# Cross network on one Trainium2 core: one layer-one chunk in two passes, bank 2 added whole, the sum over d in fp32r

## The reference

```python
x0 = xk = e                                    # (1024, 39, 16)
for W in (f0, f1, f2):
    z = einsum('bfd,bgd->bfgd', x0, xk)         # all pairs of x0 and xk
    xk = einsum('bpd,pm->bmd', z.reshape(b, f * g, d), W)
    outs.append(xk)
z = sum(concatenate(outs, axis=1), axis=-1)     # sum over d: (1024, 384)
h = concatenate([z, dense_ctx], axis=1)
h = maximum(h @ W_top1 + b_top1, 0)
h = maximum(h @ W_top2 + b_top2, 0)
y = h @ W_top3
```

## Time and profile before

| | |
|---|---|
| median of 3 runs | 1281.71 us (1281.46 to 1281.8) |
| the profiled execution's own time | 1282.15 us |
| its span | 1280.3 us |
| PE busy | 1247.0 us, 97% |
| DVE busy | 1038.5 us, 81% |
| POOL busy | 951.5 us, 74% |
| ACT busy | 751.1 us, 59% |

### The profile page before, as it was taken

How to read it: one execution, slowest core, us unless ns; L and a number is a source line. 1 busy time by engine, 2 the same in 40 slices (tenths; PEclk the granted TensorE clock), 3 DMA queues, 4 the chain that set the end, 5 groups by cost and what they waited for, 6 DMA issues and landing times.

```text
span 1280.3 us, 19891 instructions
## 1 busy us (share of the span) xinstructions
PE 1247.0 (97%) x5493; PEld 963.6 (75%) x5493; DVE 1038.5 (81%) x3346; ACT 751.1 (59%) x2422; POOL 951.5 (74%) x844
## 2 busy tenths in 40 slices
PE   1999999999999999999999999999999999999999
PEld 0677778777787778777787777877787777877765
DVE  4789896898868996889969888699978898788830
ACT  4456664666646665666646666466656666466641
POOL 6578886788868886788868888588867888675640
PEclk9999999999999999999999999999999999999999
DMA  7632222122212221122221222222221222111000
GB/s 174 180 102 61 66 69 61 45 54 68 62 57 69 68 60 40 50 61 68 69 54 38 68 61 66 61 68 61 53 48 51 66 69 68 47 44 50 1 1 1
DMA packets 121764, 78.69 MB, mean 61 GB/s; under 512 B 77436, under 2 KB 89826, under 8 KB 121652
## 3 DMA queue, kind: packets, MB, share of 16 engines
q1 hardware_dynamic: 107418, 73.69, 20.4%
q0 software_dynamic: 10240, 2.64, 2.4%
q10 hardware_dynamic: 3994, 1.09, 0.4%
HBM read 18.50 MB, written 2.63 MB: 16 GB/s over the span
## 4 chain that ended last, share of the span: by engine, by line
PE 97%; DMA 1%; POOL 1%; issue 0%; ACTq 0%; ACT 0%; DVE 0%; SPq 0%
PE ps L499 23%; PE ps L503 22%; PE ps L500 22%; PE ps L479 14%; PE ps L526 6%; PE ps L515 5%; PE ps L582 2%; PE ps L592 1%; PE ps L462 1%; POOL x_in L393 1%; DMA x_in<-in_tables,row_at 0%; PE ps L599 0%; ACTq L272 0%; DMA x_rows<-x_in 0%; DMA ids_now<-in_ids 0%
## 5 line engine op out<-in xcount | busy, mean ns | idle before, releaser
L823 DVE SCALAR_TENSOR_TENSOR terms<-ps,x_scal,terms 128x128 f32<-128x128 f32 x2944 | 805.7, 341 | 158.4 <-ACT terms L670 94.5
L670 ACT ACTIVATE terms<-ps,x_scal 128x128 f32<-128x128 f32 x2048 | 585.3, 369 | 370.4 <-PE ps L503 363.6
L417 POOL TENSOR_TENSOR terms<-terms 128x1024 f32<-128x1024 f32 (+2 forms) x384 | 577.4, 1504 | 178.5 <-DVE terms L823 156.3
L499 PE MATMUL ps<-w_high,x_high 128*128 128x512 f32 (+1 forms) x1280 | 581.7, 454 | 2.9 <-DVE x_low L801 2.9
L503 PE MATMUL ps<-w_high,x_low 128*128 128x512 f32 (+1 forms) x1280 | 496.1, 388 | 0.0
L500 PE MATMUL ps<-w_low,x_high 128*128 128x512 f32 (+1 forms) x1280 | 494.3, 386 | 0.0
L393 POOL DMA_INDIRECT x_in<-in_tables,row_at x320 | 305.2, 954 | 81.5 <-issue 65.1
L499 PEld LDWEIGHTS ps<-w_high,x_high 128*128 128x128 f32 x1280 | 240.6, 188 | 82.9 <-issue 20.6
L500 PEld LDWEIGHTS ps<-w_low,x_high 128*128 128x128 f32 x1280 | 241.1, 188 | 77.8 <-issue 29.8
L503 PEld LDWEIGHTS ps<-w_high,x_low 128*128 128x128 f32 x1280 | 240.1, 188 | 50.5
L479 PE MATMUL ps<-prods,w 117*128 117x512 f32 x262 | 136.1, 604 | 5.2 <-DVE prods L789 5.0
(11 more groups left out here) (48 smaller groups left out, 412.7 us busy)
## 6 DMA issues: line engine op xcount, KB each, us to landing
prods<-x_cols SPq DMA_DIRECT2D x189, 234.0 KB
x_cols<-x_rows SPq DMA_DIRECT2D x96, 78.0 KB
x_first<-x_cols SPq DMA_DIRECT2D x95, 78.0 KB
x_in<-in_tables,row_at POOLq DMA_INDIRECT x320
x_diag<-x_scal SPq DMA_DIRECT2D x256, 9.8 KB
x_rows<-x_in SPq DMA_DIRECT2D x32, 80.0 KB
s<-in_f SPq DMA_DIRECT2D x3, 832.0 KB, 11.6
wt<-in_W_top SPq DMA_DIRECT2D x1, 768.0 KB
```

Of the source, the lines that this page charges most:

```text
L417: nc.gpsimd.tensor_tensor(t[:, 0:n], t[:, 0:n], t[:, n:2 * n], ALU.add).then_inc(s_tree, 1)
L499: nc.tensor.matmul(y, x1_high[:, par, at:at + P], high, start=True, stop=False)
L670: op = nc.scalar.activation(terms[:, u % 2, FB * ACT_BANKS.index(q) + i, :], ps[:, (BANKS * u + q) % RING, i * G:(i + 1) * G], ACT.Copy, s ...
L823: nc.vector.scalar_tensor_tensor(out=acc, in0=y, scalar=x0, in1=acc, op0=ALU.mult, op1=ALU.add).then_inc(s_mac, 1)
```

## The change

It does four things.

1. One chunk of layer one, number 1 (`REST`), becomes a chunk of 78 rows: the order of shifts is changed (`SHIFT_OF`) so that it is the one whose third part is empty. Its high part fills rows 0 to 77 of a tile `rest`; the free 39 rows take half of its low part, moved there by a DMA that ACT issues (`move_rest`), first one half, then the other. Two fp32r passes then give all three products: weights high over high with half of the low part below, then weights low over high with the other half. The chunks 2, 3 and 4 are split in three passes, 0, 5 and 6 stay fp32; before it was 1, 2, 3 and 0, 4, 5, 6.
2. Bank 2 (`SHARED`) is scaled by ACT in place, in PSUM, and DVE adds the whole bank, 512 columns, onto four accumulators (`add_shared`), placed behind bank 4's multiply-adds (`ADD_AT`). DVE now has 19 multiply-adds in four chains and one add a tile, ACT 20 scalings.
3. The places of products, high halves, low halves and chunks are new, and there is one more high and low half in a group.
4. The sum over d becomes three fp32r passes. x2 is split, high by ACT behind bank 7, low by DVE behind bank 8 of the next tile; the x0 scalars are split once a group, and the diagonals hold both parts.

The prologue gets the weights of the two-pass chunk (with two DMAs on SP) and the split of the first scalars; in the tail ACT also splits the last x2.

```diff
-DVE_BANKS = tuple(q for q in range(BANKS) if q not in ACT_BANKS)
-CHAINS = 2
+SHARED, ADD_AT = 2, 4
+SCALED_BANKS = tuple(sorted(ACT_BANKS + (SHARED,)))
+DVE_BANKS = tuple(q for q in range(BANKS) if q not in SCALED_BANKS)
+DVE_ORDER = tuple(k for q in DVE_BANKS for k in ((q, SHARED) if q == ADD_AT else (q,)))
+CHAINS = FB
...
-SPLIT = (1, 2, 3)
+SHIFT_OF = (0, KT - 1) + tuple(range(1, KT - 1))
+REST, SPLIT = 1, (2, 3, 4)
+KH = (SPT - 1) * F
...
+X2_HIGH, X2_LOW = 7, 8
+SPLIT_SCALARS = (0, 5)
+PRODUCTS = ((0, 2), (0, 4), (0, 9), (1, 4), (2, 2), (2, 4), (3, 1))
+HIGHS = ((0, 6), (1, 2), (1, 6), (2, 5))
+LOWS = ((0, 7), (1, 6), (1, 8), (2, 7))
+MOVE_LOWS = ((0, 8), (1, 3))
+CIN1 = ((0, 6), (1, 3), (1, 9), (2, 1), (2, 4), (2, 8), (3, 1), (3, 4))
+CIN1_OF = (0, REST, 2, REST, 3, 5, 4, 6)
...
 def move_diag(gf, j):
-    sp.wait_ge(s_scal, gf + 1)
+    sp.wait_ge(s_scl, gf + 1)
...
+    sp.wait_ge(s_w0l, 1)
+    for i in range(2):
+        sp.dma_start(w0_rest[KH:KR, i, :].bitcast(F32), w0_rest[i * F:(i + 1) * F, 0, :].bitcast(F32)) \
...
 def cin1(gf, n, first=False):
+    elif k == REST:
+        pe.wait_ge(s_wrest, 32)
+        pe.wait_ge(s_rest, (gf - 1) * 32 + half * 16 + 16)
+        passes = ((w0_rest[:, half, :], rest[:, :]),)
...
 def cin2(bt, u, q, scalars_next):
-        pe.wait_ge(s_mac, bt * (STEPS * MACS) + macs_before(old + 1) + CREDIT_MAC)
+        pe.wait_ge(s_mac, bt * (STEPS * MACS) + added_through(old) + CREDIT_MAC)
...
 def sum_s3(bt, u):
-    pe.wait_ge(s_x2, bt * STEPS + u - 1 + CREDIT_X2)
+    pe.wait_ge(s_x2h, bt * STEPS + u - 1)
+    pe.wait_ge(s_x2l, bt * STEPS + u - 1)
...
-    nc.tensor.matmul(ps[:, S3_BANK, 0:TB * FX], x2[:, u % 2, :],
+    nc.tensor.matmul(s3_sum, x2_high[:, :], high, start=True, stop=False)
+    nc.tensor.matmul(s3_sum, x2_high[:, :], low, start=False, stop=False)
+    nc.tensor.matmul(s3_sum, x2_low[:, :], high, start=False, stop=True).then_inc(s_s3, 1)
...
 def step(bt, u, last):
+    if q == X2_HIGH and bt + u > 0:
+        split_x2_high(bt, u)
...
+    if front and now == MOVE_LOWS[0]:
+        act.wait_ge(s_low, (gf - 1) * (NS + 1) + 1)
+        move_rest(act, 0)
+    if front and now == MOVE_LOWS[1]:
+        act.wait_ge(s_cin1, gf * SLOTS + REST_SLOTS[0] + 1)
+        move_rest(act, 1)
...
+def add_shared(bt, u):
+    dve.wait_ge(s_ya, bt * (STEPS * NA) + scaled_through(BANKS * u + SHARED) + CREDIT_A)
+    dve.wait_ge(s_mac, bt * (STEPS * MACS) + added_through(BANKS * u + ADD_AT) + CREDIT_MAC)
+    acc = terms[:, u % 2, 0:FB, :].rearrange("p t g -> p (t g)")
+    nc.vector.tensor_tensor(acc, ps[:, (BANKS * u + SHARED) % RING, :], acc, ALU.add).then_inc(s_mac, 1)
...
 def step(bt, u, last):
+    if q == ADD_AT:
+        add_shared(bt, u)
+    if q == X2_LOW and bt + u > 0:
+        split_x2_low(bt, u)
```

More of the change, by code:

```diff
@@ L360, in _ @@
             next_cols(1, 1)
+            sp.wait_ge(s_w0l, 1)
+            for i in range(2):
+                sp.dma_start(w0_rest[KH:KR, i, :].bitcast(F32), w0_rest[i * F:(i + 1) * F, 0, :].bitcast(F32)) \
+                    .then_inc(s_wrest, 16)
             move_seconds(1, 1)
[L362 to L366, removed]
+            sp.wait_ge(s_ones, 2)
+            sp.wait_ge(s_scl, 1)
+            put_diag(0)
             load_late()
@@ L477, in cin1 @@
                     passes = ((w0[:, k, :], prods[0:KR, k, :]),)
-                for n, (w, x) in enumerate(passes):
-                    mm = nc.tensor.matmul(ps[:, X1_BANK, :], w, x, start=(k == 0 and n == 0),
-                                          stop=(k == KT - 1 and n == len(passes) - 1))
+                for i, (w, x) in enumerate(passes):
+                    mm = nc.tensor.matmul(ps[:, X1_BANK, cols], w, x, start=(k == 0 and i == 0),
+                                          stop=(n == SLOTS - 1 and i == len(passes) - 1))
                 mm.then_inc(s_cin1, 1)
@@ L514, in sum_s3 @@
                     pe.wait_ge(s_r, bt * 2 + CREDIT_R)
[L515 to L517 removed]
+                s3_sum = ps[:, S3_BANK, 0:TB * FX]
+                high, low = (x0_diag[:, j % 2, i, t].rearrange("p b f -> p (b f)") for i in range(2))
+                nc.tensor.matmul(s3_sum, x2_high[:, :], high, start=True, stop=False)
+                nc.tensor.matmul(s3_sum, x2_high[:, :], low, start=False, stop=False)
+                nc.tensor.matmul(s3_sum, x2_low[:, :], high, start=False, stop=True).then_inc(s_s3, 1)
             def cin3(bt, lo, hi):
@@ L708, in prologue @@
                 act.wait_ge(s_w0s, 1)
+                nc.scalar.activation(w0_rest[0:KH, 0, :], w0[0:KH, REST, :], ACT.Copy).then_inc(s_w0h, 1)
                 for i, k in enumerate(SPLIT):
@@ L739, in step, with store_h1 @@
                     store_r(bt)
-            def store_h1(h):
-                for c, bank in enumerate(L1_BANKS[h]):
+            def store_h1(h, banks=range(H1 // P)):
+                for c in banks:
+                    bank = L1_BANKS[h][c]
                     act.wait_ge(s_h1, 4 * h + c + 1)
```

177 lines of the change are left out of this document (120 added, 57 removed).

## The result

The changed kernel takes 1295.12 us (median of 4 runs, 1294.13 to 1295.54), the kernel before on the same chip 1281.76 us (1281.46 to 1282.13): 13.4 us more, a ratio of 1.0103 with a 95% interval of 1.0086 to 1.0121. It is slower by 1%, inside the forecast's range of 1258 to 1299, but 11.7 us above the forecast time of 1283.4.

A forecast was written before the change was run, and what follows sets the result against it. PE's own list of passes was taken as the bound. Terms: -27.4 saved, +17.0 add wait, +10.4 chunk 2's wait, +0.5 prologue, +1.2 tail, sum +1.7 on 1281.7: 1283.4 us; range 1258 to 1299.

The forecast's parts named there:

- likeliest case: Whole kernel: savings and new waits sum to +1.7 us, 1283.4 us; own range 1277 to 1291, chance 0.50.
- rival B: DVE's low halves end late when a GpSimd sum runs, mean over 0.85 us: 1289 to 1306 us; chance 0.16.
- C: Moved low halves reach the two-pass chunk late, each half microsecond costing 15 us: 1290 to 1305 us; chance 0.10.
- the one on the prologue: Prologue: a second scalar copy (0.30) and a weight copy (about 0.25) on ACT's path to the first chunk, +0.5 us.
- The savings: PE's passes: two-pass chunk saves 0.41 in 31 groups (-12.7 us), sum over d 0.115 a tile (-14.7 us).
- The wait for the add: Bank 7 waits 0.47 us for DVE's whole-bank add where no chunk covers it, 36 places: +17.0 us.
- Chunk 2's wait: In tile 1, second of a group's four, chunk 2 waits 0.45 us for DVE's low half, 23 places: +10.4 us.
- Groups with the last layer: In 7 groups the last layer stands between and covers chunk 2's wait for its low half.
- The tail: Last tile: the sum over d follows bank 9 directly and waits for DVE's x2 low, +1.2 us.
- A: Both waits of tile 1 don't show: 1256 us, or 1270 with both halved; chance 0.24.
- Work beside other work: ACT's some 2 us a tile fit into 2.8 it waited for PE; DVE's work nets to about zero a group.

The follow-up runs named there:

- the run with all waits out: Kernel without whole-bank add, group 0's split scalars in their own place, plus chunk 2 behind bank 0 of tile 2 and weight load cut in three: 1259.91 us.

## Why the prediction was right, and what in it was wrong

- **Faster or slower.** The forecast's likeliest case was +1.7 us, with more chance on slower than on faster. It was slower, inside the range but outside the likeliest case's own 1277 to 1291. That the range held it is luck: its upper end made room for rivals B and C, and the loss came from neither of them as they were priced. The direction does not hang on group 0's wait: with it taken out the kernel is still 3.7 us slower than the one before on that chip, 1.0030 (1.0019 to 1.0041).
- **The step that failed** is the one on the prologue: "+0.5 us", together with "SP issues as many diagonal DMAs as before, with twice the rows, a group ahead of their use". That is true of PE's use (no row of the changed kernel has PE waiting for a diagonal), and it missed a second user: ScalarE's next store needs the split scalars' single buffer free, so in group 0 it waits for those DMAs. The forecast put this wait at nothing, though the changed kernel has it (`act.wait_ge(s_diag...)` in `store_scalars`). Group 0 measured +12.7; the runs give the wait 7.0 added to the kernel before and 9.2 taken from the changed one. Without it the changed kernel takes 1286.0, 2.6 us from the forecast. The two copies for which the +0.5 stood do not show: up to the turn that begins group 0 the two traces differ by -0.05, where executions differ by more than 1 us.
- **The savings.** The two-pass chunk and the sum over d were priced at 0.87 a group; the group in which nothing waits shows 34.39 against 35.29, 0.90. The passes of 320 columns start 0.14 to 0.15 apart, on the line through 384 and 512 columns. The Trainium skill's rule in "VectorE: DVE Perf Modes", section on the TRN2 errata, gave 0.136, an estimate; the rows above differ from it, and the measurement decides.
- **The wait for the add**, 0.47 in 36 places: 0.45 in the row above and up to 0.49 elsewhere, in 34 places, some 16 us. In the last group, which has no chunks, a tile takes 7.64 us, and 7.12 in the run with all waits out: 0.52.
- **Chunk 2's wait**, 0.45 in 23 places: 0.32 in 16 plain groups, 0.51 in one, 0.74 to 0.82 in the six behind the last layer, some 10 us. With the wait for the add that is 26 to 27 us in tile 1, where the sum had 27.4. The two sizes lie near the two ends of the 0.33 to 0.70 given for it, the larger by rival B's mechanism. In the groups behind the last layer GpSimd first numbers the next batch's rows; GpSimd and VectorE there:

```profile
402.11 0.27 POOL L426 TENSOR_TENSOR row_at<-ids_now,ids_base 128x40 uint32<-128x40 uint32 x1 [1.50 <-DMA x_in<-in_tables,row_at]
402.46 4.90 POOL L455 TENSOR_TENSOR terms<-terms 128x1024 f32<-128x1024 f32 x3
```

```profile
405.66 1.10 DVE L882 TENSOR_TENSOR prods_low<-prods,prods_high 117x512 fp32r<-117x512 f32 x1
```

  GpSimd's sums start 1.5 us late, and the low half that falls into them takes 1.10 instead of 0.68, as one did before. In the last batch, where no rows are numbered, the group behind the last layer takes 35.19 like a plain one. The traces show the mechanism closely: in the changed kernel all 15 low halves over 0.8 us start while an instruction of GpSimd's sum runs and end 0.54 to 0.55 behind the end of that instruction, as all 24 of the kernel before do. So a low half waits out what is left of it; the longest took 1.86, in the run with chunk 2 later. Fourteen in the later runs that start within 0.07 us of the instruction's start take no longer than usual, and no run moves GpSimd's sums to test it. The exclusion that the Trainium skill states in "SBUF — State Buffer", section "Who interferes with whom", agrees with these rows.
- **Groups with the last layer**: chunk 2's wait is covered there, as forecast.
- **The tail**, +1.2 for the last tile: a wait of 0.94 and a slower restart are there, 1.1 in all, but what ends it is ScalarE's high part of x2, not VectorE's low part:

```profile
1240.24 0.38 PE L568 MATMUL ps<-x_diag,x_high 128*128 128x320 f32 x1 [0.94 <-ACT x_high L741]
```

- **Rivals.** A fell: both waits show. B's mechanism held in 6 groups, 2.3 us in all, but not its sign: the low halves' mean is 0.74 us, not over 0.85, against 0.78 before. C fell in the steady state, where the moved halves are in time; it came true once, in group 0, by a load that the forecast had not set beside it.
- **Work beside other work**: VectorE did not become the bound, even with bank 2 back on it (33.13 of 34.50). The whole-bank add bought time on an engine that still had some.

## What to carry to other kernels

When a change adds a buffer, ask who must wait before it is written again, and read that wait in the prologue as well as in the steady state: a transfer that is a group early later on can be the last thing in the queue at the start. When an instruction is moved, look at what is queued behind it on its engine, since one product behind a wait cost more here than the wait that the move removed. Cut the trace at a row that comes once a loop and compare the pieces: one table showed that the loss was in one of 32 groups.

## What the runs showed that was not expected

A pause of PE can cost more than its length. Behind the pauses of 4.96, 6.20 and 2.44 us the granted clock of the next stretches was 0.58, 0.50 and 0.62, and behind 3.50 us, in the run with bank 2 summed as before, 0.57; where it was at its lower level of 1.2 GHz, passes over 512 columns took 0.43 instead of 0.23. Behind pauses of 1.59 and 1.83 us, in the run with the scalars' own place, and behind one of 2.19, in the run with the add behind bank 1, it stayed at 1.00. No run varies one pause by itself, so what decides between the two stays open. The moved low half, a DMA of 78 KB, landed 7.0 us after its issue while the weight load ran.
